# Second row tile's variances from ScalarE's running sums instead of VectorE's statistics

## The reference

```python
def _layernorm(x, axis=-1, eps=1e-05):
    m = jnp.mean(x, axis=axis, keepdims=True)
    v = jnp.var(x, axis=axis, keepdims=True)
    return (x - m) / jnp.sqrt(v + eps)
...
        scores = jnp.einsum('lnc,lmc->lnm', q, q) / scale
        prob = jax.nn.softmax(scores, axis=-1)
        msg = jnp.einsum('lnm,lmc->lnc', prob, q)
        return x + jnp.transpose(msg, (1, 2, 0))
...
        g = jnp.einsum('bsh,mh->bsm', x, Wg)
        u = jnp.einsum('bsh,mh->bsm', x, Wu)
        h = jax.nn.silu(g) * u
        return jnp.einsum('bsm,hm->bsh', h, Wd)
...
    x = x + _L0_attn_ref(_layernorm(x, axis=-1))
    x = x + _L0_ffn_ref(_layernorm(x, axis=-1), L0_ffn_gate_q, L0_ffn_gate_absmax, L0_ffn_up_q, L0_ffn_up_absmax, L0_ffn_down_q, L0_ffn_down_absmax)
```

## Time and profile before

| what | us |
|---|---|
| median of 3 runs | 1668.28 (1667.95 to 1668.56) |
| the profiled execution | 1667.4 |
| its span, first to last instruction | 1665.7 |
| TensorE busy in the span | 1630.1 (98%) |
| VectorE busy | 1202.4 (72%) |
| ScalarE busy | 1030.1 (62%) |
| GpSimd busy | 59.8 (4%) |

### The profile page before, as it was taken

One profiled execution on the slowest core, in us unless ns is written; L12 is line 12 of the kernel. 1 busy time (PEld: TensorE's weight loads), 2 busy tenths in 40 slices (PEclk: granted clock), 3 DMA queues, 4 the chain that ended last, 5 costly groups with the idle time before them and its releaser, 6 DMA issues.

```text
span 1665.7 us, 20171 instructions
## 1 busy us (share of the span) xinstructions
PE 1630.1 (98%) x7888; PEld 786.5 (47%) x7888; DVE 1202.4 (72%) x1540; ACT 1030.1 (62%) x1118; POOL 59.8 (4%) x98
## 2 busy tenths in 40 slices
PE   6889999999999999999999999999899999999999
PEld 6865444444444444444444444444344444444444
DVE  7888967685766767576686767678777767577566
ACT  5679676776766667676666767688786526352000
POOL 4261000000000000000000000000000000000000
PEclk9999999999999999999999999999999999999999
DMA  6340232331422233142233314243764444343773
GB/s 269 114 165 14 95 120 95 120 139 52 161 91 104 95 121 139 51 164 95 96 103 112 140 51 165 95 151 100 258 249 176 150 150 175 125 175 126 254 258 123
DMA packets 76895, 226.39 MB, mean 136 GB/s; under 512 B 5248, under 2 KB 19968, under 8 KB 76288
## 3 DMA queue, kind: packets, MB, share of 16 engines
q1 hardware_dynamic: 76800, 225.10, 37.7%
HBM read 156.93 MB, written 68.16 MB: 135 GB/s over the span
## 4 chain that ended last, share of the span: by engine, by line
PE 93%; DVE 3%; ACT 2%; issue 1%; DMA 1%; POOL 0%; SPq 0%; DVEq 0%; POOLq 0%
PE ps L1553 20%; PE ps L1555 20%; PE ps L1554 20%; PE ps L1691 10%; PE ps L1692 10%; PE ps L1693 10%; PE ps L1523 2%; DVE stats L938 1%; PE ps L1532 1%; ACT codes L641 1%; PE ps L1509 0%; DMA codes<-q_dram 0%; DMA xa<-x_dram 0%; ACT xa L691 0%; POOL ln_scale L572 0%
## 5 line engine op out<-in xcount | busy, mean ns | idle before, releaser
L641 ACT ACTIVATE codes<-codes 128x1024 f32<-128x1024 f32 (+1 forms) x672 | 708.1, 1055 | 153.8 <-DMA codes<-q_dram 139.9
L1386 DVE SCALAR_TENSOR_TENSOR xb<-ps,y_back,xb 128x512 f32<-128x512 f32 x140 | 103.9, 749 | 73.5 <-PE ps L1693 68.9
L1553 PE MATMUL ps<-xa,wg 128*128 128x512 f16 x388 | 147.0, 379 | 1.1 <-issue 1.1
L1553 PE MATMUL ps<-xb,rw 128*128 128x512 f16 x388 | 147.1, 379 | 0.7 <-ACT gs L723 0.7
L1553 PE MATMUL ps<-xa,rw 128*128 128x512 f16 x388 | 147.1, 379 | 0.0
L1554 PE MATMUL ps<-xa,rw 128*128 128x512 f16 x388 | 147.1, 379 | 0.0
L1555 PE MATMUL ps<-xa,rw 128*128 128x512 f16 x388 | 147.1, 379 | 0.0
L1553 PE MATMUL ps<-xb,wg 128*128 128x512 f16 x388 | 147.1, 379 | 0.0
L1554 PE MATMUL ps<-xb,wg 128*128 128x512 f16 x388 | 147.1, 379 | 0.0
L1555 PE MATMUL ps<-xb,wg 128*128 128x512 f16 x388 | 147.1, 379 | 0.0
L1554 PE MATMUL ps<-xb,rw 128*128 128x512 f16 x388 | 147.1, 379 | 0.0
(11 more groups left out here) (278 smaller groups left out, 2914.3 us busy)
## 6 DMA issues: line engine op xcount, KB each, us to landing
codes<-q_dram SPq DMA_DIRECT2D x84, 512.0 KB, 4.6
absm<-a_dram SPq DMA_DIRECT2D x69, 512.0 KB, 3.7
h_dram<-rw SPq DMA_DIRECT2D x28, 1024.0 KB, 4.2
gs<-h_dram SPq DMA_DIRECT2D x21, 1344.0 KB, 5.9
h_dram<-rw SPq DMA_DIRECT2D x28, 768.0 KB, 4.6
rw<-h_dram SPq DMA_DIRECT2D x11, 896.0 KB, 5.8
rw<-x_dram SPq DMA_DIRECT2D x16, 512.0 KB, 11.0
xa<-a_dram SPq DMA_DIRECT2D x13, 512.0 KB, 5.4
```

The costliest lines, as they stand in the source:

```text
L641: fn(real, real if step else whole, ACT.Prelu, bias=at0, scale=slope, alpha=left).then_inc(bends_done, 1)
L1386: return v.scalar_tensor_tensor(out=dst, in0=ps[:, bank, :], scalar=y_back[:, 0:1], in1=dst, op0=ALU.mult, op1=ALU.add)
L1553: mm(dst, w_hi, x_hi, start=(start and kt == 0), stop=False, skip_group_check=True)
```

## The change

VectorE no longer takes the statistics of row tile 1: 8 `row_stats` and 4 small aggregations go. ScalarE reads tile 1 twice instead. `row_total(n)` passes over a whole row (1024 numbers) of batch entry n with an accumulating output, four times, behind each second `copy_yt` of tile 3; a small instruction turns the four sums into minus the means. `square_total(n)` passes over the same row with minus the mean as bias and squares it, again accumulating, four times, behind `x_blocks(1)`, `(3)`, `(5)` and `(7)`. What both write besides the sums goes to an unused part of the weights' memory. Built, each of the eight passes is two ScalarE instructions, the pass and one that reads the accumulator and signals. GpSimd's factors for tile 1 wait for the fourth sum of squares, and are four instructions instead of five.

```diff
--- before.py
+++ after.py
@@ -201,6 +201,9 @@
         stats = sb("stats", [P, B, 2, 6], F32)
         mean_var = sb("mean_var", [P, 2, B, 2], F32)
         var_eps = sb("var_eps", [P, B], F32)
+        row_sum = sb("row_sum", [P, B], F32)
+        less_mean = sb("less_mean", [P, B], F32)
+        square_sum = sb("square_sum", [P, B], F32)
         minus_half = sb("minus_half", [P, B], F32)
         plus_half = sb("plus_half", [P, 2], F32)
         ln_scale = sb("ln_scale", [P, 2, B], F32)
@@ -244,6 +247,9 @@
         norm_root = sem("norm_root")
         v_chain = sem("v_chain")
         stats_ready = sem("stats_ready")
+        sums_done = sem("sums_done")
+        mean_done = sem("mean_done")
+        squares_done = sem("squares_done")
         p_chain = sem("p_chain")
         ln_first = sem("ln_first")
         ln_ready = sem("ln_ready")
@@ -560,7 +566,7 @@
 
             def norm_factors(c, gain, rows=range(B), done=ln_ready):
                 t, at = c % 2, slice(rows.start, rows.stop)
-                pool.wait_ge(stats_ready, B * c + rows.stop)
+                pool.wait_ge(stats_ready, B * c + rows.stop if c <= CT else B * (c - 1) + rows.stop)
                 if c in (2, 3):
                     pool.wait_ge(y_act, 2 * (c - 1))
                     pool.wait_ge(y_dve, c - 1)
@@ -611,7 +617,13 @@
             pool.wait_ge(t_done, CT * LG)
             for k in range(8):
                 normalized(k)
-            norm_factors(CT + 1, 256.0)
+            pool.wait_ge(squares_done, B)
+            pool.wait_ge(ln_ready, CT + 1)
+            link(g.tensor_scalar(var_eps[:, :], square_sum[:, :], 1.0 / L, 1e-5, ALU.mult, ALU.add))
+            link(g.tensor_tensor(ln_scale[:, 1, :], var_eps[:, :], minus_half[:, :], ALU.pow))
+            link(g.tensor_scalar(ln_scale[:, 1, :], ln_scale[:, 1, :], 256.0, None, ALU.mult))
+            g.tensor_tensor(ln_bias[:, 1, :], less_mean[:, :], ln_scale[:, 1, :], ALU.mult).then_inc(ln_ready, 1)
+            pool.wait_ge(ln_ready, CT + 2)
             for k in range(8, 16):
                 normalized(k)
             norm_factors(CT + 2, 256.0)
@@ -663,6 +675,29 @@
                 rows = slice(LB // 2 * f, LB // 2 * (f + 1))
                 act.wait_ge(diff_ready, f + 1)
                 fn(prob[:, rows, :], scores[:, rows, :], ACT.Exp, bias=0.0, scale=float(C) ** -0.5).then_inc(exp_ready, 1)
+
+            unused = w_gu[0][:, 0, :, 4:6, :].rearrange("p s b t -> p s (b t)")
+
+            def row_total(n):
+
+                if n == 0:
+                    act.wait_ge(x1_ready, 2 * LG)
+                else:
+                    act.wait_ge(sums_done, n)
+                fn(unused, acc[1][:, n, :].rearrange("p (s t) -> p s t", s=2), ACT.Copy, bias=0.0, scale=1.0,
+                   accum_out=row_sum[:, n:n + 1]).then_inc(sums_done, 1)
+                if n == B - 1:
+                    act.wait_ge(sums_done, B)
+                    fn(less_mean[:, :], row_sum[:, :], ACT.Copy, bias=0.0, scale=-1.0 / L).then_inc(mean_done, 1)
+
+            def square_total(n):
+
+                if n == 0:
+                    act.wait_ge(mean_done, 1)
+                else:
+                    act.wait_ge(squares_done, n)
+                fn(unused, acc[1][:, n, :].rearrange("p (s t) -> p s t", s=2), ACT.Square, bias=less_mean[:, n:n + 1],
+                   scale=1.0, accum_out=square_sum[:, n:n + 1]).then_inc(squares_done, 1)
 
             def x_tile(k):
                 return ps[:, 5 + k % 3, :].rearrange("p (k t) -> p k t", t=P)
@@ -786,8 +821,12 @@
                     w_high(1)
             for g in range(LG):
                 copy_yt(3, g)
+                if g % 2:
+                    row_total(g // 2)
             for k in range(8):
                 x_blocks(k)
+                if k % 2:
+                    square_total(k // 2)
             bends(3, range(0, 2))
             for n in range(B):
                 x_blocks(8 + 2 * n)
@@ -940,12 +979,15 @@
 
             def row_sums(c, rows=range(B)):
                 dve.wait_ge(v_chain, chained[0])
-                if c >= 2:
+                if c == CT + 2:
+                    dve.wait_ge(ln_ready, CT + 1)
+                elif c >= 2:
                     dve.wait_ge(ln_ready, c - 1)
+                order = c if c <= CT else c - 1
                 for n in rows:
                     v.bn_aggr(mean_var[:, c % 2, n, :],
                               stats[:, n, :, :].rearrange("p a b -> p (a b)")).then_inc(stats_ready, 1)
-                dve.wait_ge(stats_ready, B * c + rows.stop)
+                dve.wait_ge(stats_ready, B * order + rows.stop)
 
             def y_row(c):
                 dve.wait_ge(ln_ready, c + 1)
@@ -1255,9 +1297,10 @@
                 dve.wait_ge(x1_ready, LG * c)
                 for g in range(LG):
                     add_message(c, g)
-                    row_stats(CT + c - 1, g)
-                row_sums(CT + c - 1)
+                    if c == 1:
+                        row_stats(CT, g)
                 if c == 1:
+                    row_sums(CT)
                     weight_low(1)
             for g in range(LG):
                 x_low(g)
```

## The result

The changed kernel takes 1671.12 us (median of 22 runs, 1668.84 to 1671.96) against 1668.44 us before (22 runs beside them, 1666.62 to 1669.76). The ratio of the two is 1.0014 with a 95% interval from 1.0008 to 1.0021, so +2.3 us (1.3 to 3.5); the medians lie 2.7 us apart. The forecast was 1670.4, with 1669.0 to 1672.2 as its range and "within 0.2%" as its likeliest verdict; both hold. What follows shows the forecast mechanism at work, with a delay of 1.85 us where 2.1 was forecast, and that most of the rest goes with TensorE's granted clock, for whose fall I had given a chance of 0.07.

A forecast was written before the change was run, and what follows sets the result against it. TensorE was taken to bound the kernel, the change acting only on when its block from 165 us begins. +2.2 at half(0)'s second group less 0.1 gave +2.1, forecast 1670.4 us, range 1669.0 to 1672.2.

The forecast's parts named there:

- The path changes over: Inside half(0): GpSimd's wait for the fourth square makes tile 1's transposes late, taking over from half(0)'s later start.
- the contention with `scale_codes(2)`: GpSimd's tile 1 half rows run beside this VectorE instruction; one may take 1.0 us more, the sum stays.
- VectorE's relief: Rival: sooner additions let TensorE run ahead through tile 2's messages, at most 0.70 and 1.00 us gained, 1666.6; chance 0.03.
- the read of the accumulator: On ScalarE: 0.19 us per read, entering five times; its costlier rival reaches 0.2% at 0.43 us a read, chance 0.12.
- The 0.1 given back: Before half(1): VectorE's tile 2 statistics, only 1.1 late, no longer stand in the way of x_low(8); -0.1 us.
- The cover ahead of `w_high(2)`: GpSimd ends tile 2 at 122.7, w_high(2) stands near 125.7; 3 us left, so GpSimd's lateness there costs nothing.
- The first term: Ahead of x_blocks(0): the fourth row pass and small instruction free ScalarE at 93.25 instead of 92.96; +0.3 us.
- ScalarE's waits vanish: Over tile 0's eight copies, ScalarE's waits of some 0.25 us for TensorE ahead of each disappear; x_blocks(7) ends 1.06 later.
- VectorE would keep up: Ahead of half(0): TensorE's and VectorE's steps between copies, done in 2.7 to 2.8 us, fit a round of 3.17.
- the second group of `half(0)`: Second term: transposes of k = 8 and 9 end at 110.2 instead of ahead of 108.04; +2.2 us, containing the first term.
- the clock's rival: Rival: TensorE's new gaps at and inside half(0) lower the granted clock once, 1.7 us lost, 1672.1; chance 0.07.
- signs of being wrong: Read above 0.4 us, clock under 1.00 between 100 and 125 us, factor stretched by VectorE, half(1) shifted unlike the second group.

The follow-up runs named there:

- removal: Changed kernel without ScalarE's passes, tile 1 normalized with tile 0's mean and variance; 1668.55 us, ratio 1.0000 to the kernel before.
- passes-kept kernel: Kernel before with VectorE's statistics kept, plus ScalarE's row and square passes whose sums nobody uses; 1669.20 us, ratio 1.0007.
- the wait alone: Changed kernel without ScalarE's passes, tile 0's statistics for tile 1, GpSimd's factors waiting until ScalarE has copied out tile 0; 1668.44 us, ratio 1.0001.
- early: Changed kernel with passes moved forward: six behind copies of tile 3's transposes, two squares behind x_blocks(1) and x_blocks(3); 1669.64 us, ratio 1.0008.
- rows only: Kernel before with VectorE's statistics kept, plus ScalarE's four row passes and the means' small instruction, no squares; 1668.64 us, ratio 1.0002.
- half(0) fill: Changed kernel with five unused 128x512 matmuls in TensorE's wait ahead of half(0), none ahead of half(1); 1670.86 us, ratio 1.0012.
- `half(1)` fill: Ten unused 128x512 matmuls in TensorE's wait ahead of half(1); added to the kernel before 1667.99 us (0.9995), to the changed kernel 1669.78 us (1.0008).

## Why the prediction was right, and where it was not

**Right by position.** The removal is worth nothing (0.08 us, ratio 1.0000). GpSimd's factors end a wait for ScalarE, at T0 + 13.65; forecast 106.1, which is T0 + 13.8. The path changes over, as forecast, from `half(0)`'s start to the second transpose inside it, as the passes-kept kernel shows by leaving exactly that part out. GpSimd's half rows of tile 1 took 7.00 us instead of 6.02, so the contention with `scale_codes(2)` was there (that instruction took 1.61 us instead of 1.27) and cost nothing that the positions show. By `half(1)` the schedule is 1.85 late; forecast 2.1. Two of the rivals are out by this: VectorE's relief brings nothing, and the read of the accumulator is far from the 0.43 us that its rival needed. The 0.1 given back between the second group and `half(1)` came (1.97 and 1.85), though tile 2's statistics still stood in the way of `x_low(8)`: it starts at 112.35, right behind them, and its copy was there at 111.41. They only no longer hold the transposes. The cover ahead of `w_high(2)` was 2.1 us (GpSimd ends tile 2 at 124.29, `w_high(2)` starts at 126.36) and not 3, and sufficed.

**Terms that were off.** The read of the accumulator claims 0.09 us of ScalarE and not 0.19: I took its duration (which is 0.19) for its claim, and forgot that it overlaps both neighbours, as the passes and copies in its rows do. Over four squares this is 0.4 too much, over the three ahead of `x_blocks(7)` 0.3. The first term, +0.3 for the row pass, was 0.10. Against that, I had let all of ScalarE's waits vanish; two of them stay (0.25 and 0.16 us, ahead of `x_blocks(1)` and `x_blocks(5)`). So ScalarE's last copy came 0.94 us late behind T0, where 1.06 stood. The rest of `half(0)`'s delay I had put at nothing, since VectorE would keep up. But its last `x_low` starts 0.27 behind that copy's end (105.83 and 105.56) instead of 0.04: it still had the `x_low` and the addition ahead of it to do. So `half(0)` moved by 1.16 where 1.06 stood, and the second group of `half(0)` by 1.97 where 2.2 stood. That these sizes come so near the forecast is in part luck: four errors of 0.2 to 0.4 us, two of each sign, nearly cancel.

**The step that failed.** "Through the 2.45 us at 121.16 the clock stayed at 1.00" was read from one execution and held against the clock's rival, which got 0.07. In the changed kernel it fell right behind that wait, and a clock under 1.00 ahead of 125 us was one of the forecast's own signs of being wrong (it averaged 0.63 in the microsecond from 124). The one execution was not typical. In the seven traces without any fill (the two kernels, the removal, the wait alone, the passes kept, early, and rows only) the clock is low in three places only, and what it takes there comes in steps of about 1.7 us of work. Here are these places in the kernel before and in the changed one:

```profile
44.00:60.00 16.00, 12.95 (x99) 11.73 (x98) 13.56 (x31) 11.25 (x18) 3.68 (x2) 0.89 0.09 36
118.00:132.00 14.00, 10.59 (x61) 5.99 (x60) 9.42 (x17) 13.19 (x19) 4.52 (x8) 1.00 0.11 37
1168.00:1190.00 22.00, 17.36 (x74) 7.33 (x72) 14.58 (x19) 15.45 (x18) 0.00 (x0) 0.92 0.64 229
```

```profile
44.00:60.00 16.00, 12.42 (x84) 11.43 (x84) 13.52 (x28) 10.75 (x18) 3.69 (x2) 0.79 0.12 45
118.00:132.00 14.00, 11.55 (x56) 6.01 (x55) 10.35 (x19) 12.87 (x19) 9.09 (x14) 0.88 0.13 41
1168.00:1190.00 22.00, 17.30 (x70) 7.23 (x69) 13.88 (x19) 15.59 (x17) 0.00 (x0) 0.84 0.72 255
```

The length of a window times what the clock lacks to 1.00 is the work lost: 1.8, 0 and 1.8 us before, 3.4, 1.7 and 3.5 with the change. The mean clock of an execution counts these steps: two make 0.998, five 0.995. It stands on record for 91 more executions of the kernel before, on three chips, and for the 22 of the changed one:

| mean clock | kernel before: executions, median us | changed kernel: executions, median us |
|---|---|---|
| 0.998 and above | 11, of which 9 at 0.998: 1667.27 | 4: 1669.20 |
| 0.997 | 28: 1668.14 | 3: 1670.06 |
| 0.996 | 49: 1668.83 | 1: 1670.02 |
| 0.995 | 3: 1670.51 | 14: 1671.48 |

So the profile that the forecast was read from, at 0.998, is of a kind that only 11 in 91 executions are. The rival was also wrong about its own cause: not the new gaps but the old wait does it, as the half(0) fill and the row-only kernel show, and the `half(1)` fill takes about one step from both kernels.

**How much is the clock's in the difference.** Low clocks are more frequent with the change: 14 of 22 executions at 0.995 against 3 of 91, and, both on one chip, 6 of 11 for the half(0) fill, whose schedule is the changed kernel's, against one of 33. At the same mean clock the two kernels lie 1.9 us apart (0.998 and 0.997; the other two rows have one and three executions on one side). By the means (1668.51 and 1670.77) the difference is 2.3 us and the mean clocks are 0.9965 and 0.9959, two thirds of a step. At 0.7 us for a step, the price of the fall at `half(1)`, that is about 0.5 us, an estimate; 1.8 remain, and the schedule says 1.85. The medians, 2.7 apart, show more of it because most of the changed kernel's executions have the lowest clock. Open is at which wait the change makes a fall longer or more frequent. It is not the one ahead of `half(1)` alone: with that one filled, the changed kernel's mean clock is still lower than the kernel before's (0.9969 and 0.9976, with 11 executions each). That the time of 1671.12 came within 0.7 us of 1670.4 is then luck in part: the schedule cost less than forecast, and the clock, which had no place in the sum, added to it.

**The profiled spans, 4.2 us apart,** add up as 0.87 ahead of T0 (the attention's clock), 1.85 the schedule, 0.68 the clock behind `half(1)`, and 0.8 at and behind the long wait that ends at 1177.63, where the clock averaged 0.73 over the 8 us from 1178; before it was 0.57 over the 4 us from 1174 and 1.00 behind them. The schedule is less than half of it.

## What to carry to other kernels

Work that is removed from an engine that waits behind it anyway brings nothing, and the engine that takes it over pays from the first instruction that stood on the path: ask of the receiver, not of the giver, where its waits lie, and put the work there (half of this change's cost on the schedule, 0.91 of 1.85 us, went by moving passes forward). Compare two traces from a common instruction up to which the change has moved nothing, since what happens before it can differ by more than the change is worth. And one execution's granted clock is one draw: where TensorE has waits like these of 2.45 to 4.7 us, compare the mean clocks and the spread of many executions, and try matmuls nobody needs in the wait.

## What the hardware showed that was not expected

An accumulating ACTIVATE is two instructions here, the pass and a read of 0.19 to 0.24 us, but the pair claims only 0.09 us more than the pass alone (1.13 us for a 128x1024 square with a per-partition bias). The clock after a wait differed between kernels with an identical schedule up to 0.1 us: 1.00 and 0.56 behind the same 2.45 us. It was lost in steps of about 1.7 us of work, so that an execution's mean clock of 0.995 to 0.998 tells how many falls it had. With unneeded matmuls in three waits of 2.45 to 4.64 us the granted clock was 1.000 and the kernel 1.9 us faster, 0.14%, with runs within 0.75 us of each other but for one. And the fall at `half(1)` cost less than the slowed matmuls suggest, since TensorE would have waited there anyway: 1.7 us of lost work became 0.67 to 0.68.
